# A graph network on one core: the attention rounds in stretches of ten tiles over three PSUM banks instead of chunks of four inside degree parts

## What is computed

```python
h = (x @ W_lin).reshape(n, H, C)
alpha = a_src[src2] + a_dst[dst2] + a_e
alpha = jnp.where(alpha >= 0, alpha, NEG * alpha)
m = jax.ops.segment_max(alpha, dst2, num_segments=n)
ex = jnp.exp(alpha - m[dst2])
denom = jax.ops.segment_sum(ex, dst2, num_segments=n)
w = ex / denom[dst2]
msg = h[src2] * w[:, :, None]
out = jax.ops.segment_sum(msg, dst2, num_segments=n)
```

## Time and profile before

| | us |
|---|---|
| timed runs, median of 3 | 7507.04 |
| profiled execution, first to last instruction (span) | 7447.1 |
| gathers of the attention stage, first start to last start | 6017.8 to 7352.9 |
| DVE busy, whole span | 3315.8 (45%) |
| POOL busy, whole span | 4460.6 (60%) |

### The profile page before, as it was taken

How to read it: one execution, slowest core, us unless ns; L and a number is a source line. 1 busy time by engine, 2 the same in 40 slices (tenths; PEclk the granted TensorE clock), 3 DMA queues, 4 the chain that set the end, 5 groups by cost and what they waited for, 6 DMA issues and landing times. The chain is left out here.

```text
span 7447.1 us, 57775 instructions
## 1 busy us (share of the span) xinstructions
PE 2431.1 (33%) x12640; PEld 1798.8 (24%) x12640; DVE 3315.8 (45%) x12439; ACT 1771.2 (24%) x5753; POOL 4460.6 (60%) x4570
## 2 busy tenths in 40 slices
PE   5776654666566610000000003555545400000000
PEld 4555544444444410000000002333333200000000
DVE  2333333333343543444444685455555433434466
ACT  1111111111111101222222225666666400000011
POOL 5666664667776655555554435666666657566545
PEclk7677776767787755555555556777777755555555
DMA  4333335665555431111111103333333332122111
GB/s 101 100 99 102 102 98 99 208 185 168 167 166 166 112 87 37 37 37 37 37 37 35 32 18 98 90 95 98 95 93 98 96 84 54 43 51 51 44 33 36
DMA packets 404927, 637.51 MB, mean 86 GB/s; under 512 B 148580, under 2 KB 248966, under 8 KB 404340
## 3 DMA queue, kind: packets, MB, share of 16 engines
q0 software_dynamic: 175664, 424.09, 22.2%
q1 hardware_dynamic: 139076, 115.67, 5.9%
q10 hardware_dynamic: 89856, 94.18, 3.9%
HBM read 529.65 MB, written 103.93 MB: 85 GB/s over the span
## 5 line engine op out<-in xcount | busy, mean ns | idle before, releaser
L1590 POOL DMA_INDIRECT mb_rows<-x_tab,mb_idx x882 | 832.1, 943 | 877.7 <-ACT mb_ps L1638 585.2
L2532 POOL DMA_INDIRECT gt_rows<-h_tab,gt_idx x882 | 847.5, 961 | 497.4 <-issue 269.8
L977 POOL DMA_INDIRECT s_rows<-y_split,srcS x824 | 854.4, 1037 | 418.7 <-issue 226.3
L2035 POOL DMA_INDIRECT eq_ring<-fx_tab,srcS x824 | 816.9, 991 | 441.7 <-issue 235.3
L555 POOL DMA_INDIRECT s_rows<-in_x,srcS x824 | 780.6, 947 | 439.1 <-issue 221.2
L2070 ACT ACTIVATE eq_ring<-eq_ring 128x64 f32<-128x64 f32 x3328 | 860.1, 336 | 442.6 <-issue 332.5
L2111 PE MATMUL eq_ps<-eq_ring,eq_onehot 128*128 128x320 f32 x1664 | 629.3, 538 | 609.8 <-issue 451.0
L1700 PE MATMUL mb_ps<-ident,mb_rows 128*128 128x128 f32 x49 | 12.4, 340 | 1857.5 <-ACT mb_rows L1667 1853.0
L2111 PEld LDWEIGHTS eq_ps<-eq_ring,eq_onehot 128*128 128x128 f32 x1664 | 381.4, 239 | 837.6 <-issue 769.6
L1055 PE MATMUL s_ps<-s_onehot,s_rows 128*128 128x128 bf16 x4992 | 460.1, 253 | 222.6 <-issue 204.7
L194 DVE TENSOR_TENSOR s_onehot<-iota,dstM 128x512 bf16<-128x512 f32 x206 | 142.2, 691 | 743.3 <-PE s_ps L1055 388.3
(11 more groups left out here) (507 smaller groups left out, 5727.7 us busy)
## 6 DMA issues: line engine op xcount, KB each, us to landing
w_tab<-s_wrow ACTq DMA_DIRECT2D x208, 264.0 KB
eq_ring<-w_tab SPq DMA_DIRECT2D x208, 264.0 KB
s_es<-in_side ACTq DMA_DIRECT2D x208, 136.0 KB
mb_rows<-x_tab,mb_idx POOLq DMA_INDIRECT x882
gt_rows<-h_tab,gt_idx POOLq DMA_INDIRECT x882
s_rows<-in_x,srcS POOLq DMA_INDIRECT x824
s_rows<-y_split,srcS POOLq DMA_INDIRECT x824
eq_ring<-fx_tab,srcS POOLq DMA_INDIRECT x824
```

The costliest lines, as they stand in the source:

```text
L977: pool.indirect_dma_start(rows[:, n % SLOTS, :], None, t["ys"], bass.IndirectOffsetOnAxis(ap=s["srcS"][:, n:n + 1], axis=0)).then_inc(gath ...
L1590: pool.indirect_dma_start(rows[:, r, n, :], None, t["x1"], bass.IndirectOffsetOnAxis(ap=idx[:, r, n:n + 1], axis=0)).then_inc(gathered[r][ ...
L2035: pool.indirect_dma_start(frow[:, n % SLOTS, :], None, features, bass.IndirectOffsetOnAxis(ap=s["srcS"][:, n:n + 1], axis=0)).then_inc(gat ...
L2532: pool.indirect_dma_start(rows[:, r, n, :], None, flat, bass.IndirectOffsetOnAxis(ap=idx[:, r, n:n + 1], axis=0)).then_inc(gathered[r][g], 16)
```

## The change

Inside a turn the chunks within parts are replaced by stretches ("runs") of ten tiles that ignore the parts: 0 to 9, 10 to 19 and so on, so 5 stretches for 49 tiles (four of 10 and one of 9). Each of the three loop instructions covers a whole stretch, up to 1280 columns; a product takes three neighbouring PSUM banks, banks 1 to 3 and 4 to 6 in turn. Rows are handed back to POOL by stretch: `consumed` has 5 semaphores per buffer instead of 8, every multiplication signals its stretch, and POOL waits at tiles 0, 10, 20, 30 and 40. Every addition waits for the signal of its own stretch. New is a wait in front of the multiplication of the third and later stretches: the addition of two stretches before, now signalled each time, must have read the PSUM banks that are to be written again. The gathers, the preamble, the parts, the phases and the finishes stay.

```diff
+        RUN = 10
+        RUNS = -(-TILES // RUN)
...
-        consumed = [[sem(f"consumed{r}_{g}") for g in range(NG)] for r in range(2)]
+        consumed = [[sem(f"consumed{r}_{c}") for c in range(RUNS)] for r in range(2)]
...
             for r in range(2):
-                for g in range(NG):
-                    sp.sem_inc(consumed[r][g], 1)
+                for c in range(RUNS):
+                    sp.sem_inc(consumed[r][c], 1)
...
                             for g in range(p + 1):
-                                pool.wait_ge(consumed[r][g], b + 1)
-                                pool.sem_inc(took, 1)
                                 for n in range(PART[g].start, PART[g].stop):
+                                    if n % RUN == 0:
+                                        pool.wait_ge(consumed[r][n // RUN], b + 1)
+                                        pool.sem_inc(took, 1)
                                     pool.indirect_dma_start(rows[:, r, n, :], None, flat,
...
-                made = {}
-
-                def add_up(c):
-                    g, lo, hi = CHUNKS[c]
-                    if c in last:
-                        dve.wait_ge(consumed[r][g], b + 2)
-                    else:
-                        dve.wait_ge(do.sem, made[c])
-                    return dve.tensor_tensor(acc[:, lo:hi], acc[:, lo:hi],
-                                             ps[:, 1 + c % 6, 0:(hi - lo) * D].rearrange("p (u d) -> p u d", d=D), ALU.add)
-
-                for c in range(CHUNKS_TO[p]):
-                    g, lo, hi = CHUNKS[c]
+                runs = [(c, c * RUN, min(c * RUN + RUN, T)) for c in range(-(-T // RUN))]
+                weights = lambda c, many: ps[:, 1 + 3 * (c % 2):4 + 3 * (c % 2), :].rearrange("p b n -> p (b n)")[:, 0:many * D]
+
+                def add_up(c, lo, hi):
+                    dve.wait_ge(consumed[r][c], b + 2)
+                    do.put(dve.tensor_tensor(acc[:, lo:hi], acc[:, lo:hi],
+                                             weights(c, hi - lo).rearrange("p (u d) -> p u d", d=D), ALU.add))
+                    added[c] = do.n
+
+                added = {}
+                for c, lo, hi in runs:
                     wide = [P, hi - lo, heads, cols]
                     mine = acc[:, lo:hi].rearrange(by_head, c=cols)
                     dve.tensor_tensor(mine, mine, ex[:, 0, lo:hi].unsqueeze(3).broadcast_to(wide), ALU.mult)
-                    weighted = dve.tensor_tensor(ps[:, 1 + c % 6, 0:(hi - lo) * D].rearrange("p (u h c) -> p u h c", h=heads, c=cols),
-                                                 rows[:, r, lo:hi, 0:D].rearrange(by_head, c=cols),
-                                                 ex[:, 1, lo:hi].unsqueeze(3).broadcast_to(wide), ALU.mult)
-                    if c in last:
-                        weighted.then_inc(consumed[r][g], 1)
-                    else:
-                        do.put(weighted)
-                        made[c] = do.n
+                    if c >= 2:
+                        dve.wait_ge(do.sem, added[c - 2])
+                    dve.tensor_tensor(weights(c, hi - lo).rearrange("p (u h c) -> p u h c", h=heads, c=cols),
+                                      rows[:, r, lo:hi, 0:D].rearrange(by_head, c=cols),
+                                      ex[:, 1, lo:hi].unsqueeze(3).broadcast_to(wide), ALU.mult).then_inc(consumed[r][c], 1)
                     if c == 0:
                         dve.tensor_tensor(dn, dn, ex[:, 1, 0:T], ALU.add)
                     else:
-                        add_up(c - 1)
-                do(add_up(CHUNKS_TO[p] - 1))
+                        add_up(*runs[c - 1])
+                add_up(*runs[-1])
+                do.sync()
```

More of the change, by code:

```diff
@@ L2507, in _ @@
                 for r in range(2):
-                    for g in range(NG):
-                        sp.sem_inc(consumed[r][g], 1)
+                    for k in range(RUNS):
+                        sp.sem_inc(consumed[r][k], 1)
                 sp.sem_inc(go, 1)
@@ L2619, in _ @@
             by_head = "p u (h c) -> p u h c"
-            last = [c for c, x in enumerate(CHUNKS) if c + 1 == len(CHUNKS) or CHUNKS[c + 1][0] != x[0]]
             def turn(before, p, b, r):
```

## The result

| | kernel before | changed kernel |
|---|---|---|
| median of the timed runs, us | 7508.12 (7497.33 to 7519.99, 4 runs) | 7459.12 (7453.89 to 7463.04, 4 runs) |
| ratio | 1 | 0.9935, 95% interval 0.9921 to 0.995 |
| profiled execution, us | 7499.95 (e1, span 7498.2) | 7461.11 (span 7459.4) |
| attention stage, first gather to end of the span, us | 1434.9 (e1) | 1393.5 |

A forecast was written before the change was run, and what follows sets the result against it. The prediction took the attention stage as bound by waits, with DVE paced at about 1.40 us an instruction setting the 49-tile phase's end. Terms -144 + 10 + 22 + 0 + 6 - 12 + 7 - 4 = -115 gave 7392 us, range 7342 to 7450.

The forecast's parts named there:

- term 1: Twelve turns of 49 tiles: gathers bind instead of DVE, 715 instead of 859.1 us, minus 144, plus 10 for slower gathers.
- the gathers' pace: POOL in the 49-tile turns: 1.25 us a tile, possible slowing to 1.40 costed at 10 us, at most 72.
- Term 4: Second finish, 39.9 us with 16 gathers beside it: some 10 more gathers, plus 6 us (0 to 20).
- Term 2: First finish (group 0), 30.0 us: gathers now run beside it, 52 us within 30 to 69, plus 22.
- Gathers at 1.40: Rival, chance 0.13: POOL alone falls to 1.40 us a gather from the 200th, adding 62 us; 7454 us.
- The pacing is not in the timed runs: Rival, chance 0.14: DVE and POOL's common step exists only in the profiled execution; 7495 to 7525 us, say 7508.
- Wide instructions stop POOL: Rival, chance 0.07: POOL can't issue during wide DVE instructions, a 49-tile gather takes 82 us; about 7580 us.
- pacing by instruction: DVE in the attention stage: one instruction per about 1.40 us, whatever its size; a 29-instruction turn takes 41 us.
- no stalls in front of the additions: 49-tile turns: DVE idle in front of L2635 for gathers instead of L2656, the addition, where it stood 396 us.
- the new wait on the addition two stretches back: In front of the third and later multiplications: 7 us a turn at most, still hidden behind the 61.3 us gather.
- The later hand-back in the small phases: Turns of 17 tiles and fewer: tile 0 free up to 2.2 us later, 0 to 33 us, taken at nothing.
- term 7: Turns of 17 tiles and fewer: a few chunks less in each, minus 4 us; last finish stays.

The follow-up runs named there:

- e1: The kernel before, unchanged, traced once more; profiled execution 7499.95 us, attention stage 1434.9 us.
- e2: Changed kernel with DVE's instructions left out in the twelve 49-tile turns, its waits and signals kept; stage 1393.3 us.
- e13: The changed kernel again, unchanged, on another chip; median 7454.04 us, 0.9935 of the kernel before, stage 1393.1 us.
- e12: Changed kernel with stretches of twelve tiles and wide mean and variance instructions in the first three finishes; 7448.36 us, 0.9922 of the kernel before.
- e7: Changed kernel with stretches of four tiles instead of ten, 53 DVE instructions a 49-tile turn; 7451.47 us, 0.9995 of the kernel before.
- e3: Changed kernel with 30 one-column fills added to each DVE turn of 49 tiles; stage 1399.4 us.
- e8: Changed kernel with mean and variance of the first two finishes taken by wide instructions; 0.9952 of the kernel before, stage 1391.7 us.
- e4: Changed kernel with 30 one-column copies added to ACT's work in each 49-tile turn; stage 1395.3 us.

## Why the prediction was wrong

The sign and the mechanism of the first step were right, the size was not: 115 us forecast, 49 measured (in the stage 41.4, by e1 and the changed kernel's trace, or 35.7 by the first trace of before; the rest lies within the scatter of the runs). Term by term, e1 against the changed kernel, us:

| term | forecast | measured |
|---|---|---|
| 1, first phase, with the gathers' pace | -134 | -101.7 |
| 2, first finish | +22 | +33.1 |
| 3, two turns of 43 tiles | 0 | +2.5 |
| 4, second finish | +6 | +35.8 |
| 5, two turns of 36 tiles | -12 | -20.7 |
| 6, up to the 17-tile turns | +7 | +4.7 |
| 7, small turns and last finish | -4 | +4.9 |
| sum | -115 | -41.4 |

**The step that failed is the gathers' pace in term 1**, taken at 10 us where its bound of 72 was the nearer end: it came to 59 (733 instead of 674). The row stood there: 37 gathers in 50 us after some 200 without a break. The bound itself was counted up to the 674th gather, and this phase has 588 (12 x 49): 388 x 0.15 are 58 us, close to what came. The prediction weighed it down because 33 paced DVE instructions lay in the same window and because only 55 of 882 gathers were slow. e2 shows that DVE has no part in it, and the account offers a reason why so few were slow: after some 190 gathers 19 are unsettled, and in the kernel before POOL's waits for the hand-back came soon after and let the number fall again. The 1.25 us is not POOL's rate; it is its rate while a reserve of some 20 gathers lasts. The twelfth turn started 733 us behind the first (802.1 less 68.7), where 684 were forecast; that an unpaced turn takes 25.5 us instead of the 41 taken for it gave 15 us of these 49 back, e1's phase was 2 us longer than the first trace's, and the term lost 32.

**Term 4 was sized by the wrong neighbour.** It was costed for 10 more gathers beside the second finish. With the gathers late, all of it lies beside them or beside what is left unsettled after the last of them, at 1.40 us for each of its 53 instructions: 74.4 us, outside the bound of 20 us more. This follows from the first mistake: that gathers late by 59 us lie beside this finish was in no term. Term 2 went to 33 of its 39 us; there the prediction had gathers beside the whole finish, and took 52 us within 30 to 69 where 63.1 came.

**What bounds the kernel was misread** one level deeper. The prediction took the slow turns of DVE, 83.8 us for 60 instructions, as lost time. By the account the settling of gathers hardly ever stood idle in that phase of the kernel before (4 us up to the first finish); it stood idle behind it, from 948 to 965, 1066 to 1082 and 1157 to 1180 us, when POOL had waited for rows too long. 882 gathers x 1.40 are 1235 us; to that come 108 us in which nothing is unsettled in e1, 66 us in e13 and 53 us in e12, which puts the last gather's settling at 1343, 1301 and 1288 us. The differences, 42 and 55 us, are those of the stages (1434.9, 1393.1 and 1379.9 us). This is a way to see where the time lies and no second proof, since the account starts from when the gathers were issued. By it the change gains what POOL's longer lead takes from those idle times, not what it takes from DVE's turns. e7 shows the other side: nearly as many instructions as before, and the same idle times (947 to 967, 1068 to 1083, 1159 to 1177 us).

**The rivals.** "Gathers at 1.40" was the case, with a chance of 0.13: 7454 us forecast, 7459 measured. That its number came so near is luck: it left term 1 at -72 us, where -101.7 was measured, and the other terms at +19, where +60.3 was measured, and the two misses cancel. "The pacing is not in the timed runs" fell in the form that it had, 7495 to 7525 us: each timed run has a span of its own, some 2 us below its time, and the stage's gain is there. Of the 59.9 us between span and median, which the prediction left lying around the span, 45.5 lie ahead of the stage by e1's trace.

"Wide instructions stop POOL" is refuted for the loop's instructions by gathers that take 0.94 to 0.95 us beside them as elsewhere in the changed kernel:

```profile
6150.28 1.48 DVE L2662 TENSOR_TENSOR gt_acc<-gt_acc,gt_ps 128x1280 f32<-128x1280 f32 x1
6150.67 0.95 POOL L2535 DMA_INDIRECT gt_rows<-h_tab,gt_idx  x1 [0.30 <-issue]
```

The port pair that the Trainium skill describes (SBUF — State Buffer, SBUF: two separate sides) shows in none of these rows. (The break-even of 1.53 us a tile that the prediction gives this rival is 1.52 by its own sum.) The Trainium skill's advice that breaking instructions up may complete work sooner where VectorE isn't saturated but causes bubbles elsewhere (Perfetto Trace Analysis, Optimizing Scalar/DVE Operations) doesn't bear out here: e7, with the narrower instructions, has a ratio to before of 0.9995, the changed kernel 0.9935.

**What held:** pacing by instruction (e3), no stalls in front of the additions (1.0 us), the new wait on the addition two stretches back at nothing (DVE stood idle 0.0 us in front of L2665). The later hand-back in the small phases, also taken at nothing, lies in term 7, which came out 9 us worse than forecast; no run shows its share.

## What to carry to other kernels

A rate read from a short stretch may be the rate at which a reserve is used up; where one row shows the same work slower after a long run without a break, cost the long run by that row. If several engines fall to the same step whatever they do, look for what they share and keep an account of it over the whole stage: here, by the account, 1.40 us a gather times their number is a floor, and only the time in which nothing is unsettled can be gained. A gain in one phase counts only if the phases behind it are not held by the same thing; e8 moved a turn 44 us forward and the end by 2.

## What was not expected of the hardware

Indirect DMAs issued by POOL step at 1.25 us for about 200, then at 1.40 us, with DVE silent as well (e2), and DVE can use the rows some 2.7 us after a gather's start at either step. Meanwhile DVE and ACT complete one instruction per 1.40 us each, a fill of 0.06 us (e3) or a copy of 0.20 us (e4), after some 20 that go through at once (18 copies in e4); they do so until 1.40 us a gather have passed, up to 27 us after POOL's last issue, and then run free. Small fills on POOL take from the reserve but don't add to the 1.40 us (1.41 us a tile with one, 1.42 with three).

What the gathers and the engines share stays open, and no run varied the rows or bytes of a gather. Open too is how DVE's and ACT's own reserves fill again: in e3 DVE put 27 instructions through in 6 us at a moment when the account had gathers unsettled. All times here, those of the timed runs too, come from executions with a recorded span, so whether the recording itself causes the pacing can't be told from them.
